# Destinations counted at eight low bits, with the lists made between the counting's tiles

## The reference

```
deg = max(count of edges by destination, 1)
edge_weight = (deg[src] * deg[dst]) ** -0.5
edge_msg = relu(edge_attr @ W1e + b1e) @ W2e + b2e
agg = segment_sum((x[src] + edge_msg) * edge_weight, dst)
h = relu(((1 + gin_eps) * x + agg) @ W1n + b1n) @ W2n + b2n
out = rmsnorm(h + x) * rms_w ;  result = layernorm(x + out)
```

## Time and profile before

| | us |
|---|---|
| median of 3 runs | 1333.68 (1332.87 to 1334.81) |
| profiled execution | 1332.28 |
| its span, first to last instruction | 1330.5 |
| busy in the span: DVE | 1260.0 (95%) |
| PE | 1159.0 (87%) |
| ACT | 1072.8 (81%) |
| POOL | 971.8 (73%) |

### The profile page before, as it was taken

How to read it: one execution, slowest core, us unless ns; L and a number is a source line. 1 busy time by engine, 2 the same in 40 slices (tenths; PEclk the granted TensorE clock), 3 DMA queues, 4 the chain that set the end, 5 groups by cost and what they waited for, 6 DMA issues and landing times. The chain is left out here.

```text
span 1330.5 us, 32120 instructions
## 1 busy us (share of the span) xinstructions
PE 1159.0 (87%) x7478; PEld 848.1 (64%) x7591; DVE 1260.0 (95%) x4743; ACT 1072.8 (81%) x3857; POOL 971.8 (73%) x1281
## 2 busy tenths in 40 slices
PE   4999729999999999998798888888888888899991
PEld 2555317777777777776576666666666666678771
DVE  5999988999999999999499999999999999899997
ACT  4999505666666666666589999999999999999996
POOL 7777744777777777677777777777777702599896
PEclk9999859999999999999799999999999999999996
DMA  4999964655555555776767888878777665677654
GB/s 123 396 352 396 389 242 111 181 165 171 173 178 177 162 176 172 247 246 249 279 228 260 303 306 298 325 285 306 297 283 282 240 226 196 238 273 278 255 209 184
DMA packets 87132, 327.93 MB, mean 246 GB/s; under 512 B 24657, under 2 KB 27456, under 8 KB 62556
## 3 DMA queue, kind: packets, MB, share of 16 engines
q1 hardware_dynamic: 55832, 256.51, 51.3%
q0 software_dynamic: 29904, 69.48, 17.1%
q10 hardware_dynamic: 1268, 0.54, 0.2%
HBM read 180.14 MB, written 153.95 MB: 251 GB/s over the span
## 5 line engine op out<-in xcount | busy, mean ns | idle before, releaser
L680 POOL DMA_INDIRECT xs<-in_x,src_x x392 | 385.9, 985 | 143.0 <-issue 119.0
L706 POOL DMA_INDIRECT agg_scratch<-staged,sca_i x385 | 381.1, 990 | 121.9 <-issue 113.3
L893 ACT ACTIVATE squares<-res 128x128 f32<-128x128 f32 x784 | 290.1, 604 | 0.5 <-DVE res L1217 0.5
L1433 PE MATMUL bank<-cT,w1n 128*128 128x512 f32 x392 | 215.8, 633 | 68.0 <-ACT cT L875 67.9
L893 ACT ACTIVATION_READ_ACCUMULATOR squares<-res 128x1 f32 x784 | 256.3, 496 | 0.0
L904 ACT ACTIVATE on<-z,offset,rstd 128x128 f32<-128x128 f32 x462 | 255.8, 846 | 0.4 <-DVE offset L1183 0.4
L1410 PEld LDWEIGHTS bank<-w2n,hn 128*128 128x128 f32 x1568 | 206.5, 192 | 70.4 <-issue 64.5
L1410 PE MATMUL bank<-w2n,hn 128*128 128x128 f32 x1568 | 207.3, 275 | 4.2 <-ACT hn L880 0.7
L880 ACT ACTIVATE hn<-bank,b1n_c 128x512 f32<-128x512 f32 x196 | 191.2, 975 | 3.5 <-PE bank L1433 3.5
L1339 PE MATMUL bank<-digits,picks 128*128 128x221 f16 x1568 | 185.2, 260 | 0.0
L875 ACT ACTIVATE cT<-bank 128x512 f32<-128x512 f32 x196 | 172.3, 879 | 8.6 <-PE bank L1426 8.6
(11 more groups left out here) (179 smaller groups left out, 2348.6 us busy)
## 6 DMA issues: line engine op xcount, KB each, us to landing
agg_scratch<-zeros SPq DMA_DIRECT2D x48, 1024.0 KB
xn<-in_x SPq DMA_DIRECT2D x48, 1024.0 KB
out<-on SPq DMA_DIRECT2D x48, 1024.0 KB, 4.5
ag<-agg_scratch SPq DMA_DIRECT2D x47, 1024.0 KB, 7.0
sums_scratch<-sums SPq DMA_DIRECT2D x49, 512.0 KB
staged<-sums_scratch POOLq DMA_DIRECT2D x28, 896.0 KB
highq<-src_key_scratch SPq DMA_DIRECT2D x49, 256.0 KB, 3.7
ea<-in_edge_attr SPq DMA_DIRECT2D x42, 256.0 KB
```

Of the source, the lines that this page charges most:

```text
L680: pool.indirect_dma_start(out=xs[:, b % XS, j, :], out_offset=None, in_=x, in_offset=bass.IndirectOffsetOnAxis(ap=src_x[:, t:t + 1], axis= ...
L706: pool.indirect_dma_start(out=agg_rows, out_offset=bass.IndirectOffsetOnAxis(ap=sca_i[:, t:t + 1], axis=0), in_=staged[:, k % STAGES, j, : ...
L893: last = act.activation(squares[:, j, :], res[:, s, j, :], ACT.Square, accum_out=ssq[:, v // SPB, s * TB + j:s * TB + j + 1])
L1433: pe.matmul(ps[2 + s][:, :], w1n[:, :], cT[:, s, :], start=True, stop=True).then_inc(hn_done, 1)
```

## The change

The low part of a destination has eight bits instead of seven (`LOW` = 256) and the high part is half as wide (`HIGH` = 392). PE multiplies the step tile's two halves by the same `oh_hi`, into banks 0 and 1. The step tiles are 256 wide: ACT makes those of three tiles of a batch, DVE the fourth (as -0.5 and 0.5, with a one hot of 2 to match). There are four buffers (`CS`) instead of two, and DVE and PE run the counting written out, while ACT keeps its loop. DVE's lists and joins become generators, of which two instructions are taken per batch: `lists` (run lengths, thresholds, bias) from batch 3, `joins` (joins, candidates' parts, eps) from batch 42. PE transposes `rows_b` before batch 36. The counts are turned by four float32 matmuls, since the change across the two halves needs a second one each (`corner`). `dst_f` is made by ACT before the counting, and DVE waits for it.

```diff
-    HIGH = -(-N // P)
+    LOW = 2 * P
+    HIGH = -(-N // LOW)
     HIGH += HIGH % 2
+    CS = 4
+    LISTS_AT, TURN_AT, JOINS_AT, OPS = 3, 36, 42, 2
...
(ACT)
+            act.wait_ge(dst_in, DST_DMAS * 16)
+            act.activation(dst_f[:, :, :], dst_x[:, :, :], ACT.Copy).then_inc(dst_set, 1)
             act.wait_ge(dst_cols, 1)
             act.wait_ge(iota_set, 1)

             def count_step(b, u):
-                s = u % 2
-                need(act, counted, b - 1)
-                for j in range(TB):
-                    act.activation(steps[:, s, j, :], iota_h[:, 0:P], ACT.Sign,
+                s = u % CS
+                need(act, counted, b - CS + 1)
+                for j in range(TB - 1):
+                    act.activation(steps[:, s, j, :], iota_h[:, 0:LOW], ACT.Sign,
...
(DVE)
+            dve.wait_ge(src_cols, 2)
+            dve.wait_ge(consts, 11)
+            dve.wait_ge(dst_set, 1)
...
+            lists, joins = make_lists(), make_joins()
+
+            def count_step(b):
+                s = b % CS
+                need(dve, counted, b - CS + 1)
+                for j in range(TB):
+                    t = b * TB + j
+                    if j < TB - 1:
+                        dve.tensor_scalar(oh_hi[:, s, j, :], iota_h[:, :], dst_hi[:, t:t + 1], None,
+                                          ALU.is_equal).then_inc(high_hot, 1)
+                    else:
+                        dve.tensor_scalar(steps[:, s, j, :], iota_h[:, 0:LOW], dst_low[:, b:b + 1], 0.5,
+                                          ALU.is_ge, ALU.subtract)
+                        dve.tensor_scalar(oh_hi[:, s, j, :], iota_h[:, :], dst_hi[:, t:t + 1], 2.0,
+                                          ALU.is_equal, ALU.mult).then_inc(high_hot, 1)
+                    if j % (TB // OPS) == 0 and LISTS_AT <= b:
+                        next(lists if b < JOINS_AT else joins, None)
+
+            for b in range(BATCHES):
+                if b == TURN_AT:
+                    for _ in lists:
+                        pass
+                count_step(b)
+            for _ in joins:
+                pass
...
             dve.wait_ge(counted, BATCHES)
-            dve.tensor_copy(cnt[:, 0:512], ps[0][:, :])
-            dve.tensor_copy(cnt[:, 512:HIGH], ps[1][:, 0:HIGH - 512])
+            dve.tensor_copy(cnt[:, 0, :], ps[0][:, 0:HIGH])
+            dve.tensor_copy(cnt[:, 1, :], ps[1][:, 0:HIGH]).then_inc(cnt_ready, 1)
...
(PE)
+                    for half in range(2):
+                        last = pe.matmul(ps[half][:, 0:HIGH], steps[:, s, j, half * P:(half + 1) * P], oh_hi[:, s, j, :],
+                                         start=first, stop=end)
...
+            for b in range(BATCHES):
+                if b == TURN_AT:
+                    turn_rows()
+                count_step(b)
+            pe.wait_ge(cand_found, 1)
+            pe.matmul(ps[2][:, 0:CANDS], ones_f[:, :], cand_own[:, :], start=True, stop=True).then_inc(cand_summed, 1)
             pe.wait_ge(cnt_ready, 1)
-            pe.matmul(ps[4][:, :], change[:, :], cnt[:, 0:512], start=True, stop=True)
-            pe.matmul(ps[5][:, 0:HIGH - 512], change[:, :], cnt[:, 512:HIGH], start=True, stop=True).then_inc(cnt_turned, 1)
+            pe.matmul(ps[4][:, 0:HIGH], change[:, :], cnt[:, 0, :], start=True, stop=False)
+            pe.matmul(ps[4][:, 0:HIGH], corner[:, 0, :], cnt[:, 1, :], start=False, stop=True)
+            pe.matmul(ps[5][:, 0:HIGH], change[:, :], cnt[:, 1, :], start=True, stop=False)
+            pe.matmul(ps[5][:, 0:HIGH], corner[:, 1, :], cnt[:, 0, :], start=False, stop=True).then_inc(cnt_turned, 1)
```

More of the change, by code:

```diff
@@ L192, in build @@
         dst_step = sb("dst_step", [P, T])
+        dst_low = sb("dst_low", [P, BATCHES])
         src_key = sb("src_key", [P, T])
@@ L986, in _ @@
             pick_columns(0)
-            dve.wait_ge(dst_set, 1)
-            here, before, after = dst_f[:, :, 1:TG + 1], dst_f[:, :, 0:TG], dst_f[:, :, 2:TG + 2]
-            gidx_g, far_g, sca_g, eqn_g, new_g, fst_g, start_g, left_g, keep_g = [by_group(t) for t in temps]
-            dve.tensor_copy(gidx_g, gidx_i[:, :, :])
-            dve.memset(keep[:, :], 1.0)
-            dve.tensor_tensor(new_g, here, before, ALU.not_equal)
-            dve.tensor_tensor(by_group(cont), here, before, ALU.is_equal)
@@ L994, in _ @@
-            link(dve.tensor_tensor(eqn_g, here, after, ALU.is_equal))
-            dve.memset(keep_g[:, :, 0:1], 0.0)
-            dve.memset(by_group(cont)[:, :, 0:1], 0.0)
-            dve.tensor_scalar(far[:, :], gidx[:, :], -BIG, None, ALU.add)
-            link(dve.tensor_tensor(fst[:, :], gidx[:, :], new[:, :], ALU.mult))
-            dve.tensor_tensor_scan(start[:, :], keep[:, :], fst[:, :], 0.0, ALU.mult, ALU.max)
-            dve.scalar_tensor_tensor(sca_g, eqn_g, SKIP, here, ALU.mult, ALU.add)
@@ L1052, in _ @@
-            for k, mask in ((1, low_m), (2, up_m)):
-                for g, row in turned(k):
-                    last = dve.tensor_tensor(masked[:, g, :], row, mask[:, :].unsqueeze(1).to_broadcast([P, row.shape[1], P]),
-                                             ALU.mult)
-                link(last)
-                link(dve.tensor_reduce(segs[:, 1 + k, :], masked[:, :, :], mybir.AxisListType.X, ALU.max))
-            link(dve.tensor_tensor(masked[:, :, :], same[:, :, :], up_m[:, :].unsqueeze(1).to_broadcast([P, G, P]), ALU.mult))
@@ L1064, in _ @@
-            link(dve.tensor_tensor(start[:, :], start[:, :], left[:, :], ALU.add))
-            link(dve.tensor_scalar(length[:, :], start[:, :], -1.0, BIG + 1.0, ALU.mult, ALU.add))
-            for k in range(CANDS):
-                c = (G - 1 - k * DIGIT // SEG) * TG + k * DIGIT % TG
-                last = dve.scalar_tensor_tensor(cand_own[:, k:k + 1], gidx[:, c:c + 1], k * DIGIT + 1.0, length[:, c:c + 1],
-                                                ALU.is_equal, ALU.mult)
-            dve.memset(ones_f[:, :], 1.0).then_inc(cand_found, 1)
@@ L1326, in _ @@
-            run(pe, BATCHES, 2, count_step, peel=1)
+                    pe.wait_ge(high_hot, b * TB + j + 1)
+                    pe.wait_ge(steps_ready, b * (TB - 1) + min(j + 1, TB - 1))
+                    first, end = b == 0 and j == 0, b == BATCHES - 1 and j == TB - 1
+                    for half in range(2):
+                        last = pe.matmul(ps[half][:, 0:HIGH], steps[:, s, j, half * P:(half + 1) * P], oh_hi[:, s, j, :],
+                                         start=first, stop=end)
@@ new lines, in count_step, with turn_rows @@
+                last.then_inc(counted, 1)
+            def turn_rows():
+                pe.wait_ge(high_ready, 1)
+                pe.wait_ge(ends_ready, 1)
+                for k in range(3):
+                    for s in range(G):
+                        last = pe.transpose(ps[ROW_BANKS[k][s // TB]][:, s % TB * P:(s % TB + 1) * P], rows_b[:, k, s, :],
+                                            ident[:, :])
+                last.then_inc(ends_turned, 1)
+            for b in range(BATCHES):
+                if b == TURN_AT:
+                    turn_rows()
+                count_step(b)
@@ L1380, in join_tails @@
                           ).then_inc(tails_summed, 1)
-            pe.wait_ge(ends_ready, 1)
-            for k in range(3):
-                for s in range(G):
-                    last = pe.transpose(ps[ROW_BANKS[k][s // TB]][:, s % TB * P:(s % TB + 1) * P], rows_b[:, k, s, :],
-                                        ident[:, :])
-            last.then_inc(ends_turned, 1)
-            pe.wait_ge(cand_found, 1)
-            pe.matmul(ps[4][:, 0:CANDS], ones_f[:, :], cand_own[:, :], start=True, stop=True).then_inc(cand_summed, 1)
             pe.wait_ge(consts, 11)
```

316 lines of the change are left out of this document (203 added, 113 removed).

## The result

The changed kernel takes **1324.66 us** (median of 4 runs, 1323.54 to 1327.05), the kernel before on the same chip 1333.28. The ratio is 0.994, 95% interval 0.9928 to 0.9953: 8.6 us faster. A second series gave 1323.23 against 1331.97, 0.9937 (0.9923 to 0.9950). 12.9 us were forecast. The profiled execution took 1323.54 us, its span is 1321.8.

What follows compares the result with a forecast made beforehand. DVE and PE together bound the counting, DVE the edge stage. Counting to 174.1 us plus 7.6 starts edges at 181.7 instead of 194.64; 1332.28 - 12.9 = 1319.4 profiled, median 1320.8 us, range 1311 to 1330.

Steps and rivals of the forecast that it cites:

- 12.9 us were forecast: Start of the edge stage: 181.7 us against 194.64, 12.9 us earlier, carried whole to the end of the kernel.
- DVE's batch: Counting, per four tiles: four comparisons of 0.231 us and a step tile of 0.196 make 1.120 us, before 1.333.
- The price that was set against my rows: Counting on DVE: the skill's 58 cycles plus a quarter of the columns, an estimated 0.78 us a batch.
- the rival of the shorter counting: Counting on DVE cheaper than taken: edges up to 30 us earlier, time 1302 to 1312; chance 0.10.
- PE and ACT: Counting: PE 1.337 us a batch, nothing saved; ACT's step tiles near 0.36 us each, at most 0.5, hidden under DVE.
- The recursion: Counting, batch by batch: DVE or PE sets the pace, ending at 174.1 us; about 16 of 36.7 us moved is hidden.
- Between counting and edges: From last counting matmul to first edge matmul: 7.6 us, of which four float32 matmuls take 3.0.
- Counted ... now 199.5: POOL's last 20 early gathers follow the counting's end, 174.3 + 25.2; POOL resumes at 199.5, 11.7 us earlier.
- Its chain runs through to the first join: POOL in the edge stage: the earlier resumption carries through, first join at 612.8 us instead of 624.50.
- if SP waits on group_done: Sign of a wrong forecast: SP waiting for a join before loading the nodes' aggregates, expected at 623.8 us.
- The handover: Edges to nodes: a join landing after 13.3 us loses 2.4 us of the gain, time 1323; chance 0.06.
- The clock: PE in the counting: granted clock falls to 1.2 GHz, adding 58 us, or 1350 with half; chance 0.06.

Runs made afterwards that it cites:

- the counting alone: Changed kernel's new counting kept, but lists and joins made after the last batch, one behind the other as before; 1332.21 us, ratio 0.9993 to the kernel before.
- Without gathers: Changed kernel, but POOL begins its gathers only when the counting has ended; one run, 1453.5 us, only the counting read.
- the own comparison waited for: Changed kernel, but in each batch without list work DVE waits once for its own comparison of the tile before; 1322.69 us, ratio 0.9924.
- the four variants in which POOL is less late: Changed kernel with a waited-for memset (0.9928), a wait for DVE's own comparison (0.9924), an unwaited memset (0.9924), or POOL's gathers not gated (0.9909).
- the nine variants with the new counting: Follow-up kernels that keep the changed kernel's counting but alter DVE's waits or memsets, POOL's gate or the list work's places; ratios 0.9872 to 0.9993.

## Why the prediction was right, and where it was not

**DVE's batch, right.** 1.120 us was forecast, 1.121 measured (9 batches in 10.09 us). Three comparisons of 392 columns lie in 0.77 us, and the forms with two operations cost what the others do. The price that was set against my rows, 0.78 us a batch, is refuted, and with it the rival of the shorter counting. It came from the Trainium skill, VectorE: DVE Perf Modes, "The TRN2 errata", which says in the same place that this row comes out too short and that the fixed part measured was about 150 cycles; an estimate with that is 1.26 us a batch, so the trace lies between the two.

**PE and ACT, right.** PE 1.327 us a batch, no gain by itself (the counting alone: 0.9993). ACT's step tiles take 0.41 us each (24 in 9.92 us), 1.24 a batch, between my value of 0.36 and my bound of 0.5; PE is full beside them. Start 20.98 against 20.6; the turned rows 2.46 against 2.1.

**The recursion, right in form, 2.3 us short.** DVE in front during the list work, PE between, and about 14 us hidden, where 16 were forecast. Of the 2.3 us, 0.4 are the later start; the rest is a counting of 155.4 us in place of 153.5. Without gathers it lasts 152.3. So the mis-sized term is the gathers beside the counting, 3.1 us, which I took as nothing; the other terms together came out 1.2 us too long, which hid part of it.

**Between counting and edges, right.** Four float32 matmuls 2.9 us against 3.0; 7.3 us in all against 7.6.

**"Counted ... now 199.5", the step that failed.** It read "POOL's gathers of the last five early batches, 20 of them ... are issued only once all 98 batches are counted: 174.3 + 25.2 = 199.5". That supposes that the 116 before them are done. They were not: gather 117 went at 189.03 in place of 158.39, since one had hung for 17.94 us and others for 1.94. "Its chain runs through to the first join" held: from gather 137 to the join it is 413.3 us before, 412.4 after, 413.4 with the own comparison waited for. So the 14.9 us of lateness at 214.42 against 199.5 came out at the join nearly whole, 14.1 us late. One of the prediction's own signs of being wrong, "if SP waits on group_done", came true: SP waited 5.6 us for that join.

**The handover was named and priced at 2.4 us.** The landing time had been varied, not POOL's start. It cost SP 5.6 us. By the four variants in which POOL is less late it is worth 0.001 to 0.003 of the ratio, some 1 to 4 us. That is less than 5.6 for two reasons that the traces show: the counting ends 1.2 to 2.5 us later in them, and the first result of the nodes follows a load that the join held up by 10.3 and 10.7 us (changed kernel, twice), other loads by 11.4 to 12.2, so about 1 us is caught up.

**The clock, refuted.** The granted clock was 1.00 from 24.7 to 185.1 us, though PE was busy 24.09 of 30 us in pieces.

A sum of the parts: 12.9 forecast, less 2.0 at the edges' start, less 0.6 within the edges, less 5.6 at SP, makes the 4.7 us that SP's load is earlier. The first result of the nodes is 6.2 earlier, the last 8.7. The 2.5 us between those two are not explained. In the profiled executions the kernel before takes 31.2 us for ten of its last results (170 to 180), this one 28.3, with nothing in the change that reaches there; the variants, whose node stage is the same code, take 28.1 to 30.1. From the first result to the last, before takes 657.8 us, the changed kernel 655.2 and 654.9, the nine variants with the new counting 655.2 to 657.6. So a part of it may be that execution's.

**Luck.** The time lay within the range although the handover failed, and in part by luck. The kernel with the counting alone shows 2.5 to 4.6 us gained behind the edges' start by none of the forecast's terms. If the changed kernel has the same gain, then without it it would have been some 4 to 6 us faster than before, not 8.6 (an estimate), of the 12.9 forecast.

**How it fits what is known.** While DVE ran comparisons alone, an indirect DMA on POOL took 17.94 us in place of 0.95. The Trainium skill, SBUF — State Buffer, "SBUF: two separate sides", says that POOL writes the descriptors of such a DMA through a port pair that it shares with DVE, that DVE in a fast mode locks it out, and that the lock lasts to the end of DVE's instruction. The traces agree that DVE's comparisons hold POOL's gathers, and that a gather holds a comparison (by 0.20 us); no run here shows the ports. In length they don't fit a lock of one instruction: here the gather hung over some 80 in a row (17.94 us at 0.224). Nor do they show that such a run always holds POOL, since gathers of 1.94 and 1.03 us got out beside two others. The prediction did not weigh this rule, and the rule alone would not have told these places apart.

## What to carry to other kernels

When an edit changes the order of an engine's instructions, look at what other engines do beside it, place by place: here the same two instructions on DVE let gathers through in one place and held one for 17.94 us in another, and its cost showed 540 us later. Follow each slack that a forecast leans on (24 us on POOL) to the work that has to be done before it, and not only to its release. And try how thinly interleaved work is best spread: one piece a batch for longer was worth 8 us more than two a batch for shorter, but spreading it over nearly all batches gave 3.7 us of that back. Last, test each half of a change alone: the half that gained nothing showed that some of the gain lay outside the forecast's sum.

## What was unexpected of the hardware

- A gather of 0.95 us lasted 17.94 us beside back-to-back comparisons of float16 (392 columns), 23.35 with longer ones (782 columns); 1.6 to 2.0 when one memset of 0.06 us, or one wait of DVE for itself, came in each batch of 1.1 to 1.3 us.
- Such a run doesn't always hold POOL: with DVE busy 13.04 of 13.04 us on the same instructions, six gathers took 1.94 us each, and in the kernel before, with DVE busy 120.00 of 120, each took 1.03. What opens the way stays open. By the records it needs neither an idle moment of DVE (none beside the memset; at most 0.05 us beside list work, where gathers of 0.95 us went through) nor another kind of instruction.
- The block works both ways, unevenly: DVE started a comparison 0.20 us late, at the end of POOL's gather, but a gather that hangs costs DVE nothing (10.09 us for nine batches with and without).
